# Cross attention of a decoder kernel: key and query projections without padding columns, laid out in strips through DRAM; blank rows written a stage earlier

## What is computed

```python
x1 = layernorm(x + delta_attention(x))           # the "delta stage": conv, delta rule, gates, output projection
q = heads(x1 @ q_w + q_b) * 16 ** -0.5           # 16 heads of 16
k = heads(ctx @ k_w + k_b)
v = heads(ctx @ v_w + v_b)
o = softmax(q @ k.T) @ v                         # per batch and head, 256 x 256 scores
x2 = layernorm(x1 + o @ o_w + o_b)               # the "cross stage"
logits = x2 @ gate_w; top-2 of 8 experts; rows of x2 go to their experts' places
out = layernorm(x2 + experts(x2) + shared_experts(x2))
```

## Time and profile before

| | us |
|---|---|
| median of 3 executions | 993.73 (988.31 to 998.14) |
| the profiled execution | 993.91 |
| its span in the profile | 992.1 |
| PE busy | 880.3 (89% of the span) |
| DVE busy | 616.4 (62%) |
| ACT busy | 445.0 (45%) |
| POOL busy | 343.2 (35%) |

### The profile page before, as it was taken

One profiled execution on the slowest core, in us unless ns is written; L12 is line 12 of the kernel. 1 busy time (PEld: TensorE's weight loads), 2 busy tenths in 40 slices (PEclk: granted clock), 3 DMA queues, 4 the chain that ended last, 5 costly groups with the idle time before them and its releaser, 6 DMA issues.

```text
span 992.1 us, 18359 instructions
## 1 busy us (share of the span) xinstructions
PE 880.3 (89%) x6859; PEld 657.9 (66%) x6859; DVE 616.4 (62%) x1456; ACT 445.0 (45%) x813; POOL 343.2 (35%) x318
## 2 busy tenths in 40 slices
PE   6799789789988887899889889989998999999995
PEld 5567576667666664687556556556776777777774
DVE  5799798456888888652567776774461343333255
ACT  5687566336665554432144544445331322222221
POOL 9422201023456546332001342233540242222584
PEclk9999899768999998999799998999996999999998
DMA  5699579886545432122991112002202122221421
GB/s 166 208 271 295 167 184 267 273 221 152 107 109 116 86 59 69 54 86 103 388 376 54 63 62 79 19 23 98 80 22 82 55 65 65 65 65 49 149 64 63
DMA packets 144630, 123.53 MB, mean 125 GB/s; under 512 B 89952, under 2 KB 126752, under 8 KB 143264
## 3 DMA queue, kind: packets, MB, share of 16 engines
q1 hardware_dynamic: 141136, 112.99, 40.2%
q0 software_dynamic: 3408, 9.38, 2.5%
HBM read 74.05 MB, written 48.29 MB: 123 GB/s over the span
## 4 chain that ended last, share of the span: by engine, by line
PE 59%; DVE 16%; ACT 11%; POOL 7%; issue 4%; DMA 1%; SPq 0%; POOLq 0%; DVEq 0%; ACTq 0%
PE ps L2505 10%; PE ps L1911 5%; PE ps L2520 5%; PE ps L666 4%; DVE cross_room L1944 3%; PE ps L2369 3%; PE ps L1851 3%; PE ps L1973 2%; DVE big L1398 2%; POOL hank L345 2%; PE ps L2382 2%; PE ps L1612 2%; PE ps L423 2%; POOL kept L2652 2%; PE ps L1354 2%
## 5 line engine op out<-in xcount | busy, mean ns | idle before, releaser
L1989 ACT ACTIVATE cross_room<-ps 128x1024 f32<-128x1024 f32 x64 | 65.5, 1024 | 100.2 <-PE ps L1915 100.2
L2505 PE MATMUL ps<-wr,xbT 128*128 x312 | 101.4, 468 | 1.8 <-ACT xbT L2541 1.8
L1944 DVE TENSOR_REDUCE cross_room<-ps 128x4 f32<-128x1024 f32 x64 | 78.0, 1223 | 36.4 <-PE ps L1911 35.6
L1911 PE MATMUL ps<-kept,cross_room 32*128 32x256 f32 x512 | 75.1, 415 | 20.0 <-DVE cross_room L1944 18.5
L2594 POOL DMA_INDIRECT y_dram<-yb,dest_row x39 | 37.6, 963 | 139.4 <-DVE dest_row L2570 135.2
L2505 PEld LDWEIGHTS ps<-wr,xbT 128*128 128x128 f32 x312 | 59.9, 193 | 30.5 <-issue 4.2
L1314 POOL TENSOR_TENSOR st<-st,exponent 128x20 f32<-128x20 f32 x16 | 56.6, 3535 | 66.8 <-DVE st L1289 65.5
L1915 PE MATMUL ps<-cross_room,kept 32*128 32x256 f32 x512 | 76.2, 417 | 0.0
L1911 PEld LDWEIGHTS ps<-kept,cross_room 32*128 32x128 f32 x512 | 47.7, 193 | 38.1 <-issue 18.5
L550 DVE SCALAR_TENSOR_TENSOR room<-room 128x256 f32<-128x256 f32 x144 | 58.3, 479 | 11.3 <-ACT room L499 11.3
L2579 DVE TENSOR_TENSOR cross_room<-cross_room,ps 128x352 f32<-128x352 f32 x39 | 20.3, 521 | 61.3 <-PE ps L2505 61.3
(11 more groups left out here) (349 smaller groups left out, 2252.7 us busy)
## 6 DMA issues: line engine op xcount, KB each, us to landing
xs_dram<-params SPq DMA_DIRECT2D x17, 1040.0 KB, 17.8
room<-in_gW SPq DMA_DIRECT2D x8, 1280.0 KB, 7.8
tok_dram<-room SPq DMA_DIRECT2D x8, 768.0 KB, 6.4
fir_dram<-room SPq DMA_DIRECT2D x6, 1024.0 KB, 7.2
paths<-fir_dram SPq DMA_DIRECT2D x48, 128.0 KB, 3.7
xb<-xs_dram SPq DMA_DIRECT2D x39, 130.0 KB, 2.4
hank<-rt_dram SPq DMA_DIRECT2D x8, 512.0 KB, 7.7
yr<-y_dram SPq DMA_DIRECT2D x16, 256.0 KB, 3.6
```

Of the source, the lines that this page charges most:

```text
L1911: m1 = nc.tensor.matmul(ps[:, c, t * T:(t + 1) * T], strips(qS[b % 3], g, c)[:, t * P:(t + 1) * P], kS(b, g)[c * CH:(c + 1) * CH], start=T ...
L1944: V.tensor_reduce(mx[:, :, g, XD + 2 * h * CH:XD + (2 * h + 1) * CH + 1:CH].rearrange("p t c -> p c t"), ps[:, pair(h), :].rearrange("p c ...
L1989: S.activation(pT[g % 2][:, pair(h)].rearrange("p c k t -> p (c k t)"), ps[:, pair(h), :].rearrange("p c n -> p (c n)"), ACT.Exp).then_inc ...
L2505: m = nc.tensor.matmul(ps[:, 2 * (j % 2) + half, 0:FF], xbT[j % 2][:, k, :], wr[:, bass.ds(e, 1), k, half, :].rearrange("p e n -> p (e n)" ...
```

## The change

1. **Keys.** The projection uses 256 columns, reordered so that PSUM row (u, d, c) holds element d of head 8j+4u+c: 4 matmuls in one bank and not 8 in two, and two ACT copies and not four. They go to `staged` (two buffers). SP writes them to `k_pad` in DRAM (2 stores of 16 x 4 runs of 2 KB each) and reads them back as strips of 32 partitions (one load of 512 KB, 1 KB runs on the SBUF side).
2. **Queries.** The same with `q_pad`; scale and bias are applied by DVE in one instruction for each half. The query of batch b+1 is made in the step in which batch b has its maxima, in rounds 1 and 3, and its strips are stored and loaded in that step. The pipeline has four parts over 11 steps. The first query is made in the delta stage (`pe_turn_first`, `pe_first_query`), its strips are stored there, and loaded right after the meeting. A slot of scores waits for that load (`q_in`, `k_in`).
3. **Constant rows** of `k_pad` and `q_pad` (ones and zeros) are written in delta steps 4 to 7 from a 128 x 1024 pattern that POOL makes at the stage's start (one memset, four selects). The padded weights, their clearing and their filling on POOL go; two reordering copies on POOL come, in step 9.
4. **Blank rows** are stored from the delta stage's steps 3 to 8 (17 stores of 1,040 KB as before, in runs of 2,080 and not 4,160 bytes), three in each step, between SP's other issues.
5. PSUM banks: the table of the delta stage's end has one bank for the keys, and one each for the first query and its x1. That of the cross stage has 12 names and not 13.

```diff
+def sp_strips_out(pg, pad, staged, landed):
+    for u in range(2):
+        pg.nc.sync.dma_start(pad.rearrange("c r (u n) t -> u r c (n t)", u=2)[u][0:XD], flat(staged[HS[u]])).then_inc(*landed.up(16))
+def sp_strips_in(pg, strips, pad, landed):
+    pg.nc.sync.dma_start(strips, pad.rearrange("c r g t -> (c r) g t")).then_inc(*landed.up(16))
...
+        def sp_blank(step):
+            sp.wait_ge(s.cleared, 6 + NCH)
+            strips = NE * STRIDE // P
+            places = env.xs_dram[0:NE * STRIDE].rearrange("(p k n) w -> p k n w", p=P, n=BLANKS)
+            for k in range(step * 12, min(step * 12 + 12, strips // BLANKS), 4):
+                nc.sync.dma_start(places[:, k:k + 4], env.blank.unsqueeze(1).broadcast_to([P, 4, BLANKS, XW])).then_inc(*s.blank_out.up(16))
+                yield
+                yield
...
+        def pe_heads(name, w, src):
+            for j in range(KT):
+                for k in range(KT):
+                    m = nc.tensor.matmul(kv_bank(name)[:, j * T:(j + 1) * T], w[:, k, j * P:(j + 1) * P], src[:, k, :], start=(k == 0),
+                                         stop=(k == 1))
+            return m
...
         def act_keys(b):
-            act.wait_ge(s.cross_made, CROSS_MADE)
-            for half, name in enumerate((f"K{b}", f"k{b}")):
-                act.wait_ge(kv.k_made, 2 * b + half + 1)
-                for g in range(2):
-                    m = S.activation(env.kS(b, 2 * half + g), kv_bank(name)[:, g * T:(g + 1) * T], ACT.Identity,
-                                     bias=env.bk[:, 2 * half + g:2 * half + g + 1])
-                m.then_inc(*kv_copied(name).up())
+            act.wait_ge(s.k_made, b + 1)
+            act.wait_ge(s.blank_out, s.blank_out.made)
+            act.wait_ge(kv.k_out[b % 2], 32 * (b // 2))
+            for j in range(KT):
+                m = S.activation(env.staged[b % 2][:, j, :], kv_bank(f"K{b}")[:, j * T:(j + 1) * T], ACT.Identity, bias=env.bk[:, j:j + 1])
+            m.then_inc(*kv_copied(f"K{b}").up())
...
+        sp_beside = {3 + n: sp_blank(n) for n in range(6)} | {
+                     9: rounds({0: ((C, 0), (C, 1))}),
+                     10: rounds({0: ((C, 2), (C, 3), (X, 0)), 1: ((out, 0),), 2: ((C, 4),),
+                                 3: ((out, 1), (C, 5), (out, 2), (back, 0), (back, 1))}),
+                     11: rounds({0: ((out, 3), (X, 1), (X, 2), (X, 3), (C, 6), (sp_query, 0), (back, 2)), 1: ((C, 7),),
+                                 2: ((out, 4), (back, 3), (out, 5), (back, 4)), 3: ((out, 6),)})}
...
         def sp_queries(b):
-            if b >= 4:
-                copied(sp, "y", b - 4)
-                nc.sync.dma_start(xin[b % 4][:], batch(env.x1_dram, b)).then_inc(*x_in[b % 4].up(16))
-            yield
+            for _ in range(4):
+                yield
+            if b < B:
+                copied(sp, "q", b)
+                sp.wait_ge(kv.q_in[b % 2], 16 * (b // 2))
+                sp_strips_out(pg, env.q_pad[b % 2], env.staged[b % 2], kv.q_out[b % 2])
+                sp_query_in(b)
+            if 4 <= b + 1 < B:
+                copied(sp, "y", b - 3)
+                nc.sync.dma_start(xin[(b + 1) % 4][:], batch(env.x1_dram, b + 1)).then_inc(*x_in[(b + 1) % 4].up(16))
+            yield
...
         def pe_scores(b, slot):
...
-                copied(pe, f"q{g // 2}", b)
+                pe.wait_ge(kv.q_in[b % 2], 16 * (b // 2 + 1))
+                pe.wait_ge(kv.k_in[b % 2], 16 * (b // 2 + 1))
...
+        def sp_first():
+            sp_query_in(0)
+            sp_keys_out(pg, env, B - 1)
+            for b in range(5, B):
+                sp_keys_in(pg, env, b)
```

312 lines of the change are left out of this document (180 added, 132 removed).

## The result

| | before | changed |
|---|---|---|
| median | 989.88 (20 executions, 982.84 to 998.14) | 984.04 (20 executions, 975.97 to 992.00) |
| the profiled execution | 993.91 | 988.87 |
| its span | 992.1 | 987.1 |

The ratio is 0.9948, with an interval from 0.9925 to 0.9971: some 5 us faster, where 15 were forecast. That is within 1% of no change, and outside the likeliest case of the prediction (976 to 983), though inside its range.

What follows compares the result with a forecast made beforehand. PE was taken to bound the kernel (busy 880.3 of 992.1 us), with DVE pacing most score slots. Gains of 9.1 + 1.4 + 0 + 4.6 = 15.1 us took 993.91 to 978.8, stated as 978.7; range 970 to 991.

Steps and rivals of the forecast that it cites:

- the likeliest case of the prediction: Whole kernel: the forecast itself holds, 976 to 983 us, chance 0.42.
- Term 6: Delta stage: blank-row stores delay SP's next loads by at most 8 us, hidden in a 24 us step; cost 0.
- Term 1: Keys at the delta stage's end: 13.8 us less on PE, 9.1 us net; range 6 to 11.
- Terms 2 and 3: Cross stage's head: scores start earlier, gain 1.4 us (2 to -1); first step of maxima: 0 (+1 to -3).
- The prediction's other estimate: Query round trip in the cross stage: store 2.3 us, load 3.2 us, 5.9 us with the issue.
- Term 4: Six full cross-stage steps with a query: 0.77 of a removed query half's 1.72 us comes through each; 4.6 us.
- Term 5: Later queries' strip round trips, 6.1 us: covered by 14.9 us in full steps, 7.4 in the first; cost 0.
- The clock stays low: First cross-stage steps: lighter work and idle time keep PE at half clock for more slots; 984.5 us, chance 0.17.
- The query's strips miss the next step: First slot of each of seven cross-stage steps waits for strips; 25 us slower, 1004 us, chance 0.06.
- Blank rows and constants hold the delta stage: Six delta steps each lose more than 4 us to late loads; 25 us slower, 1004 us, chance 0.06.

Runs made afterwards that it cites:

- G: The changed kernel with blank and constant stores issued behind a step's token and inverse loads; ratios to the kernel before 0.9838, 0.9887 and 0.9843.
- experiment 15: G a third time, unchanged, on the same chip as Experiment 13 and experiments 14; ratio to the kernel before 0.9843, median 975.62 us.
- Experiment 10: G with the four key matmuls of every batch issued twice, eight a batch as in the kernel before; ratio to the kernel before 1.0044.
- experiment 4: The changed kernel run and profiled again without edits; ratio to the kernel before 0.9945, median 984.25 us.
- Experiments 9: G with only the first batch's four key matmuls issued twice; ratio to the kernel before 0.9920.
- experiments 12: G with the first batch's key matmuls twice and the cross stage's first query strips loaded in two pieces; ratio to the kernel before 0.9850.
- Experiment 13: G with the first batch's key matmuls twice and the first and second queries' strips each loaded in two pieces; ratio to the kernel before 0.9865.
- experiments 14: The kernel of experiments 12 run again without further edits; ratio to the kernel before 0.9900.
- experiment 7: The kernel before with only the blank rows moved into the delta stage, behind a step's token and inverse loads; ratio to the kernel before 0.9970.
- experiments 1: The kernel before with only the blank rows moved into the delta stage, at the places the changed kernel gives them; ratio to the kernel before 1.0008.

## Why the prediction was wrong

**Term 6, blank rows in the delta stage at 0, is the step that failed.** It cost 6.0 us in the first pair of profiles, 8.6 us of waits in the second, and some 9 us between the changed kernel and the mean of G's three series. Two things in it were wrong. "Those loads are issued for the step after, and a step is 24 us" took a step's length for the slack of a load. The trace of before had the right number: SP issues the token load at 289.40, the step that uses it begins some 16 us later (305.75). And it counted blank rows only. The constant rows (640 KB to a store pair, issued just ahead of the path loads) were in the diff and had no term. I had weighed the rival with the right mechanism, but with the point "loads later than a step", and so with 0.06. The DMA share came out between the two that I had (0.75, 1.0 at worst), 0.86: the sum over the queue was right and the question was wrong, since who stands behind whom decides. By the Trainium skill, "DMA: Bandwidth & Descriptors", section "Queues, rings and completion order", transfers issued by SP share one ring on each DMA engine and are consumed in ring order; the traces agree so far as token loads landed in 11.6 us in the median with the stores ahead of them, and in 6.8 us in experiment 15 with them behind.

**Term 1, keys: 9.1 forecast.** From the second batch's keys on it was 9.0, with the pieces right: no hole, 1.72 us for each removed group, a wait of 0.99 us ahead of the first query (1.3 forecast), context loads in time. Experiment 10 shows the price again from the other side (10.7 us). The first batch was wrong in part. I had its saved 1.7 us end in a longer wait for the context, at no price. They ended in a wait for DVE (3.15 us in the first profile, 1.87 in experiment 4). In the first profile PE was at 1.2 GHz behind it, which took 2.3 us more, and over the whole stretch the term is 6.7; in experiment 4 it stayed at 2.4 GHz, and the term is the 9 us forecast. So the first pair of profiles shows the low clock's price, and not one that every execution pays.

Experiments 9, 12, 13 and 14, which are alike at this place, speak for the idle time as the cause. Where the longest wait was 1.19 or 1.34 us, the rows behind it ran at 2.4 GHz and 23.1 and 23.2 us lay between the eighth gate mark and the second values; where it was 1.79 or 1.90, they ran at 1.2 GHz, and it was 25.3 and 25.4. Over all 17 profiles, the rows behind this place are at 2.4 GHz in the six whose longest wait is 1.48 us or less, and at 1.2 GHz in ten of the eleven where it is 1.79 or more. The eleventh is experiment 4, with 1.87. So the length of the wait alone does not decide it, and what else does is open. By the Trainium skill, "TensorE: Matmul & The Clock Gate", section "HAM oscillation — how this bites in real kernels", waits for DMAs put the array back to half clock each time; the trace agrees for the 4.73 us wait for strips (the first scores of x8 in 1.76 us, where the second group of x8 takes 1.13). It does not agree for each such wait: those of 1.19 and 1.34 us for a context load and those of 3.05 and 2.88 us for strips (experiments 12 and 13) had 2.4 GHz right behind them, and in G a wait of 1.85 us for DVE had 1.2.

**Terms 2 and 3: a gain of 1.4 forecast.** First scores came 1.1 us earlier (4.73 us behind the values and not 5.87; load 3.9 us from issue to use and not 3.5). The first step took 2.3 us more, 0 forecast. Of the round trip, 7.1 us from the first store's issue to the first score instead of 6.1, the stores were nearly as costed (2.9 us to the load's issue, 2.6 forecast) and the load took 4.2 instead of 3.5. The larger part is that the query was ready 9.1 us into the step (469.00 to 478.07) and not 6.5. The prediction's other estimate, by the Trainium skill (3.2 us for the load), rests on a section about transfers issued by GpSimd; SP issued these, and they took 3.9 and 4.2. Up to the first output projection it is 54.4 us with the old queries (experiment 7) and with the new (experiment 15), so that I put both terms together at 0. That is not free of the clock: the two halves of the first 36 us had a grant of 1.00 and 0.91 in experiment 7, 0.72 and 1.00 in experiment 15. Experiment 13 shows that a shorter trip would not have helped, DVE's reductions stand right behind.

**Term 4, six steps at 0.77: 4.6 forecast.** It is 2.8 to 2.9 us, 0.6 in each of five steps; the step lengths are 24.8, 26.6, 31.4, 26.0, 24.7 before and 24.4, 25.9, 30.7, 25.4, 24.1 after, and the two last ones are equal. The mechanism, a wait for DVE in place of part of the matmuls, is what the waits ahead of the sixth slot show, 1.11 us in four of the five steps and not 0.95. The difference is the way from DVE to PE: the forecast let the slot begin 0.01 us behind the reduction's end, and in the changed kernel it begins 0.15 us behind it (the reduction that starts at 574.05 takes 1.22 us, the slot begins at 575.42). The forecast also counted six such steps, and there are five between the marks.

**Term 5** was right for the full steps: no score waits for strips from the third step on. For the first step its "7.4 us of cover" was 4.8 (the query was late, as said).

**The sum.** 15.1 forecast, less 6.0 (term 6), 2.4 (term 1), 1.4 (terms 2 and 3) and 1.7 (term 4) leaves 3.6 us, which is also what the three marked stretches give (6.7 - 6.0 + 2.9). The profiled pair's other 1.4 us, to 5.0, are the start (+2.6), the stretch up to the first output projection (-2.2: 1.1 more to the second step's start, 3.3 less behind it, where the grant was 0.81 and not 0.62) and the end (-1.8), rows that move as much between executions of one kernel. The medians give 5.8. Against experiments 1 and 7 (0.9989 in the mean) the three series of G (0.9856 in the mean) stand at 13 us, of which the marks explain 9.6 (6.8 + 2.8). The rest is within what series of 6 to 12 executions can tell, and I leave it open.

**The rivals.** "The clock stays low" is true of some executions: over the 18 us that experiment 7's windows show, the grant was 0.62 in the kernel before and 0.91 in experiments 1 and 7, 0.81 and 0.72 in the two profiles of the changed kernel, and 1.00, 0.72 and 1.00 in the three of G. Whether the change makes it more frequent, so few profiles can't say. "The query's strips miss the next step" happened in one step of seven, at 2 us. "Blank rows and constants hold the delta stage" came with its mechanism, at a quarter of its price (6.0 us and not 25) and without a load that was late by a step. None of the others came.

## What to carry to other kernels

When stores are moved into an idle part of a queue, take from the trace the time between each load's issue and its first use, and subtract what is put ahead of it, all kinds of stores together. A queue at half its share is no cover; one position behind the urgent load made these stores free. And a matmul saved ahead of a wait can be worth less than nothing: here 1.7 us saved only made a wait longer, and in most profiles, though not in all, the clock was low behind it, at 2.3 us. What a matmul is worth also depends on its round: four of them gave 0.6 us in one round and cost 1.9 in another.

## What the runs showed of the hardware

- In the same place of a step, six path loads took 4.24 us to issue on SP in the kernel before, 6.47 behind a blank store, 9.50 behind the constant stores and 10.31 behind both. With neither directly ahead (experiment 15) it was 6.52. So these issues are no fixed cost; the constant stores ahead made them longer, and the one blank store did not by itself.
- At one place PE's rows ran at 1.2 GHz behind waits of 1.79 to 1.90 us (experiments 14, 15 and 9) and at 2.4 GHz behind waits of 1.13 to 1.48 us, but once also behind one of 1.87 (experiment 4). The low clock lasted from 3.4 us (experiment 9: L1412, 414.04 to 417.42) to 6.6 us (experiment 15, 413.23 to 419.83).
- A slot of scores began 0.15 us behind the end of the DVE reduction that it waited for (575.27 to 575.42 in the changed kernel).
- The 17 blank stores of 1,040 KB landed in 6.8 us in the median beside the delta stage's loads, against 17.8 us where they were issued back to back:

```profile
xs_dram<-staged SPq DMA_DIRECT2D x17, 1040.0 KB, 6.8
```
